# A decoder layer in float32: feed-forward loop with one cyclic order for each engine, scores of two heads as 64-row pairs in two parts, softmax by head, projections up to 1.5 tiles ahead

## Chip, cores and metric

One core of a Trainium2 chip runs the whole program. The metric is the device time of one execution in microseconds (us). Three executions of the kernel before took 1336.63, 1340.5 and 1342.84 us, median 1340.5 us.

## What is computed

Input x has 4 batch rows of 512 positions and 256 features. Three blocks with residuals follow each other: causal self-attention with 16 heads, linear cross-attention with a context, and a feed-forward block of two layers, in which each layer is local attention plus a gated MLP. Only the last block is touched here:

```python
def local_attention(q, k, v):          # windows of 128, each sees itself and the one before
    sim = jnp.einsum('bhwid,bhwjd->bhwij', bq * QK_SCALE, look_around(bk))
    sim = jnp.where(mask, -jnp.finfo(sim.dtype).max, sim)
    return jnp.einsum('bhwij,bhwjd->bhwid', jax.nn.softmax(sim, -1), look_around(bv))

def _layer(x, ...):                    # twice
    q, k, v = split(shift_token(x) @ wqkv)          # 8 heads of 64
    q, k = rotary_xpos(l2norm(q) * qs, l2norm(k) * ksc)
    x = x + local_attention(q, k, v) @ wo
    h = layernorm(shift_token(x)) * lg + lb
    a, g = split(h @ w1 + b1)                       # 2 x 682
    return x + (a * gelu(g)) @ w2 + b2
```

## The kernel before, in words

The program is one list of instructions for each engine, with semaphores between them. The feed-forward block has STEPS = 8 tiles m, one for each layer and batch row (m = 4 layer + batch row), of 512 positions in T = 4 windows t of 128. The work on a tile:

- `hT`: y transposed, split in a rounded part (`hT_hi`) and the rest (`hT_lo`), so that three fp32r matmuls give nearly a float32 product.
- `qkv` (m, t, q or k or v): one window's projection, six matmuls of 512 columns in one PSUM bank (`qkv_tile`, L1461 for all matmuls of the helper `product`). For q and k ACT squares it, DVE multiplies with the rotary tables (L1278, L1284), sums the squares (L1288) and takes a maximum (L1291), POOL adds and computes the inverse norms (L663 to L680). For v ACT copies it.
- `Tqk` (m, t): q and k transposed (L1703). ACT copies q, DVE k (`lkT`).
- `S` (unit u): scores of two heads, u = 4 m + j (`local_scores`, L1721). A head's q stands in `lqz`, [features, pair, window, head, position]: 64 rows hold the head, the other 64 are zeros that POOL sets once, so the matmul contracts over 128 rows of keys of both heads. A head's four windows fill two banks (0 and 1), and `for h`, `for k` asks for 0, 1, 0, 1. DVE adds the mask and takes the maximum (L1324), then the negated maximum (L1331).
- `exp` (u) on ACT (L912, four activations for a head), `soft` (u): DVE's reciprocals (L1337) and POOL's products (L655, L658), both heads in one item.
- `T` (u, h): probabilities transposed (L1736), in banks 3 and 4, copied out by ACT and DVE. `AV` (u): the two heads' outputs go to rows 0 to 63 and 64 to 127 of one bank (L1754), ACT copies it to `loT`.
- MLP of the tile: `wo` (two halves, L1769), `stats`, `sh` (the shifted half of y by two products, L1782, L1784), `norm` (POOL), `apply` (DVE, `hn`, L1374, L1378), `hnT` (transposes, L1793), six hidden tiles `w1` with `hid` and `gl`, and `w2` in two halves.

One table, `SLOTS`, orders all of it. It has four strings, one for each unit j of a tile, and names what comes in that unit; the MLP of tile m - 1 and the projections of tile m + 1 stand between the attention parts of tile m:

```python
SLOTS = ("wo_0 v q soft_now k wo_1 S T0 T1 stats sh norm exp AV Tqk apply bias",
         "v soft_now S hnT q k T0 hid_0 hid_1 T1 hid_2 exp Tqk AV", ...)
```

All engines walk the same list `order` (`cross`, then the slots of m = 1 to 6, then `closing`) and each does its share of an item. PSUM banks are dealt out in that order too: `turn` gives the next of a ring, banks 2, 5, 6, 7 for projections, wo, w1, w2, sh and AV, 3 and 4 for transposes. `wait_free` makes PE wait for the reader of a bank's last contents, `wait_full` a reader for PE. The weights of layer 1 are loaded in one DMA into `wqkv_next`, which shares memory with other buffers, and split on ACT and DVE (`weights`).

Of the kernel before, what the change touches and what calls it, by code (L numbers as in the profile page):

```python
# [14 lines left out]
P = 128  # L15
# [28 lines left out]
GELU_T = 2  # L44

# [35 lines left out]
def build(nc, a, out, x2_dram):  # L81

    with ExitStack() as ctx:
# [99 lines left out]
        shift = sbt(ctx, "shift", [P, 2, P])  # L183
        hn = sbt(ctx, "hn", [P, T, D])
        hnT_hi = sbt(ctx, "hnT_hi", [P, E2, S], F32R)
# [5 lines left out]
        raw = ExitStack()  # L191
        wqkv_next = sbt(raw, "wqkv_next", [P, E2, 3 * INNER])
        raw.close()
# [24 lines left out]
        lqz = sbt(ctx, "lqz", [P, FPAIRS, T, 2, P])  # L218
# [79 lines left out]
        def take(key, bank):  # L298
# [6 lines left out]
        SET1 = 3  # L305
# [4 lines left out]
        WO_PART = ("wo_0", "wo_1", "stats")  # L310
        SLOTS = ("wo_0 v q soft_now k wo_1 S T0 T1 stats sh norm exp AV Tqk apply bias",
# [3 lines left out]

        def slot(m, j):

            u = m * FPAIRS + j
            names = SLOTS[j].split()
            if m == B - 1 and j == 0:  # L320
                names = ["weights", *WO_PART] + [n for n in names if n not in WO_PART]
            if j == 0 and m % B == 1 and m > B:
                names = ["w1_parts"] + names
            items = []
            for name in names:
                if name in ("v", "q", "k"):
                    items.append(("qkv", m + 1, j, name))
                if name in ("Tqk", "Tqk_before"):
                    items.append(("Tqk", m + 1, j - (name == "Tqk_before")))
                if name == "hT" and m + 2 < STEPS:  # L330
                    items.append(("hT", m + 2))
                if name in ("S", "exp", "soft"):
                    items.append((name, u + 1))
                if name == "soft_now":
                    items.append(("soft", u))
                if name in ("T0", "T1"):
                    items.append(("T", u, int(name[1])))
                if name == "AV":
                    items.append(("AV", u))
# [5 lines left out]
                if name == "weights":  # L345
                    items.append((name, 1))
# [1562 lines left out]
```

## Time and profile before

| | |
|---|---|
| median of three executions | 1340.5 us |
| profiled execution: time | 1342.08 us |
| profiled execution: span of the instructions | 1340.3 us |
| PE, weight loads, DVE, ACT, POOL: busy share | 92%, 70%, 65%, 53%, 44% |
| mean granted clock of TensorE | 0.981 of full speed |

The span is cut up by an engine's records; a record's start and length are measured, matmuls are pipelined and overlap their neighbours, so the distance from start to start is what a matmul costs in a row of them. A float32 matmul has two records, an fp32r matmul one. "Idle before" is time in which an engine had nothing running, put down to the one that released it.

### The profile page before, as it was taken

To read this page: it belongs to the slowest core of one execution; us is meant where nothing else is said; L and a number is where in the kernel's file an instruction comes from. 1 tells how busy PE (TensorE), PEld (TensorE's weight loads), DVE (VectorE), ACT (ScalarE), POOL (GpSimd) and SP (SyncE) were. 2 spreads that over 40 slices of the span, in tenths; PEclk is the share of its full clock that TensorE was granted. 3 is DMA by queue.
4 is the path that set the end of the run, shared out by engine and by line. 5 is a ranking of instruction groups with operands and counts; after the bars stand their busy time and mean duration, and the time that the engine had idled before them with its cause. 6 is when DMAs were issued, how large, how long until landed. Compare 5 with 4: busy or idle time off the path is not lost.

```text
span 1340.3 us, 20468 instructions
## 1 busy us (share of the span) xinstructions
PE 1230.4 (92%) x6672; PEld 943.7 (70%) x6672; DVE 875.3 (65%) x2443; ACT 710.9 (53%) x1728; POOL 593.3 (44%) x649
## 2 busy tenths in 40 slices
PE   5899999999998999877799999899999899998978
PEld 4777777777776667565577867777777677776666
DVE  7677777787773656867675585665665955755341
ACT  3677667666662342535456456374465563653531
POOL 1444445444442111466655365355463653652320
PEclk9999999999999999889899999999999999999999
DMA  6222122211223100230000000100001000001010
GB/s 212 48 49 67 37 47 71 48 41 38 48 63 127 32 1 4 68 103 1 1 1 1 0 1 0 48 1 1 17 6 62 1 1 0 2 23 40 1 48 16
DMA packets 31083, 46.09 MB, mean 34 GB/s; under 512 B 4540, under 2 KB 19600, under 8 KB 30992
## 3 DMA queue, kind: packets, MB, share of 16 engines
q1 hardware_dynamic: 30992, 44.98, 11.7%
q8 instruction: 44, 0.72, 0.2%
q14 instruction: 47, 0.39, 0.1%
HBM read 24.00 MB, written 4.19 MB: 21 GB/s over the span
## 4 chain that ended last, share of the span: by engine, by line
PE 32%; issue 21%; DVE 18%; POOL 14%; ACT 13%; DMA 0%; DVEq 0%; POOLq 0%; ACTq 0%
PE psum L1461 19%; POOL probs L621 12%; ACT lp L912 7%; PE psum L1721 4%; PE psum L1754 3%; DVE ra L1278 2%; DVE lp L1324 2%; DVE rb L1284 2%; DVE ss L1288 2%; PE psum L1736 2%; PE psum L1769 1%; DVE lpT L1342 1%; PE psum L1703 1%; ACT sq L897 1%; DVE ss L1291 1%
## 5 line engine op out<-in xcount | busy, mean ns | idle before, releaser
L621 POOL TENSOR_TENSOR probs<-probs,rden 128x128 f32<-128x128 f32 (+3 forms) x256 | 177.4, 729 | 211.7 <-DVE rden L1056 211.7
L912 ACT ACTIVATE lp<-lp,lneg,rn 128x256 f32<-128x256 f32 (+1 forms) x256 | 143.3, 562 | 36.3 <-DVE lneg L1331 36.2
L778 ACT ACTIVATE probs<-probs,negmax 128x128 f32<-128x128 f32 (+3 forms) x256 | 140.6, 554 | 22.6 <-DVE negmax L1051 22.6
L1721 PE MATMUL psum<-lkT,lqz 128*128 128x256 f32 (+1 forms) x512 | 119.4, 375 | 19.9 <-DVE lmax L1324 17.6
L1721 PEld LDWEIGHTS psum<-lkT,lqz 128*128 128x128 f32 x512 | 83.0, 195 | 49.5 <-DVE lmax L1324 38.4
L663 POOL TENSOR_TENSOR ra<-ra,rb 128x512 f32<-128x512 f32 x32 | 42.5, 1327 | 156.6 <-DVE rb L1284 156.6
L1324 DVE CUSTOM_DVE_ANT_0 lp<-psum,local 128x256 f32<-128x256 f32 (+1 forms) x256 | 87.1, 385 | 37.4 <-PE psum L1721 36.3
L1044 DVE CUSTOM_DVE_ANT_0 probs<-psum,causal 128x512 f32<-128x512 f32 (+3 forms) x256 | 110.0, 486 | 2.2 <-issue 1.1
L667 POOL TENSOR_TENSOR rn<-ss,neg_half 128x8 f32<-128x8 f32 x64 | 105.4, 1647 | 5.5
L658 POOL TENSOR_TENSOR lp<-lp,lrden 128x768 f32<-128x768 f32 x64 | 97.6, 1524 | 0.0
L743 ACT ACTIVATE lpT<-psum 128x512 f32<-128x512 f32 x64 | 38.4, 600 | 105.6 <-PE psum L1736 105.6
L1461 PE MATMUL psum<-q,k_rest 128*128 128x256 f32 (+2 forms) x256 | 88.4, 357 | 4.6 <-DVE rowmax L1044 3.0
L1527 PE MATMUL psum<-ident,probs 128*128 128x128 f32 x640 | 90.7, 273 | 1.7 <-POOL probs L621 1.6
L1736 PE MATMUL psum<-ident,lp 128*128 128x128 f32 x448 | 68.3, 287 | 22.1 <-DVE lpT L1342 9.9
L1461 PE MATMUL psum<-hnT_lo,w_hi 128*114 128x512 f32 (+1 forms) x192 | 80.2, 418 | 7.6 <-DVE hnT_lo L1310 7.1
L1461 PE MATMUL psum<-w,hid 114*128 114x256 f32 (+1 forms) x384 | 85.4, 379 | 1.1 <-DVE hid L1388 1.1
L655 POOL TENSOR_TENSOR lp<-lp,lrden 128x128 f32<-128x128 f32 x64 | 25.6, 400 | 137.0 <-DVE lrden L1337 137.0
L1461 PE MATMUL psum<-wqkv_hi,hT_lo 128*128 128x512 f32 x192 | 82.3, 429 | 0.7 <-ACT oxT L743 0.7
L1736 PEld LDWEIGHTS psum<-ident,lp 128*128 128x128 f32 x448 | 53.7, 146 | 39.4 <-DVE lpT L1342 14.5
L1461 PEld LDWEIGHTS psum<-w,hid 114*128 114x128 f32 (+1 forms) x384 | 71.8, 190 | 11.2 <-DVE hid L1388 1.5
L1527 PEld LDWEIGHTS psum<-ident,probs 128*128 128x128 f32 x640 | 74.1, 141 | 6.8 <-POOL probs L621 2.1
L1461 PE MATMUL psum<-q,k 128*128 128x256 f32 (+2 forms) x256 | 78.6, 324 | 0.0
(165 smaller groups left out, 3128.1 us busy)
## 6 DMA issues: line engine op xcount, KB each, us to landing
k<-k_round SPq DMA_DIRECT2D x128, 128.0 KB, 2.4
x<-in_x SPq DMA_DIRECT2D x8, 512.0 KB, 6.1
aw<-in_w_quads SPq DMA_DIRECT2D x4, 768.0 KB, 5.0
w_raw<-in_w SPq DMA_DIRECT2D x2, 1364.0 KB, 6.5
ctxT<-in_ctxT SPq DMA_DIRECT2D x4, 512.0 KB, 3.6
x_scratch<-x SPq DMA_DIRECT2D x4, 512.0 KB, 3.7
x<-x_scratch SPq DMA_DIRECT2D x4, 512.0 KB, 5.6
wqkv_raw<-in_wqkv SPq DMA_DIRECT2D x1, 1536.0 KB, 10.1
```

The lines of the kernel that those rows point to most:

```text
L621: ins = pool.tensor_tensor(pr, pr, rden[:, j % 2, h, i:i + 1].broadcast_to([P, TRI[i]]), ALU.mult)
L658: pool.tensor_tensor(pr, pr, r, ALU.mult).then_inc(l_prob, 1)
L663: pool.tensor_tensor(q3, q3, rb[:, 0, :], ALU.add).then_inc(l_q, 1)
L667: pool.tensor_tensor(rn[:, m % 2, t, i, :], ss[:, i, :], neg_half[:, 0:FH], ALU.pow).then_inc(l_rn, 1)
L778: ins = act.activation(pr, pr, ACT.Exp, bias=negmax[:, j % 2, h, i:i + 1], scale=ADH ** -0.5, accum_out=den[:, j % 2, h, i:i + 1])
L912: ins = act.activation(pr, pr, ACT.Exp, bias=lneg[:, u % 2, h, w:w + 1], scale=rn[:, m % 2, w, 0, 2 * j + h:2 * j + h + 1], accum_out=lden ...
L1044: ins = dve.tensor_tensor_reduce(probs[:, j % 2, h, TRI_AT[i]:TRI_AT[i + 1]], bank[:, at:at + TRI[i]], causal[:, S - TRI[i]:S], 1.0, -3e38 ...
L1324: ins = dve.tensor_tensor_reduce(lp[:, u % 2, h, lo:hi], bank[:, at:at + hi - lo], local[:, LOC - (hi - lo):LOC], 1.0, -3e38, ALU.add, ALU ...
L1461: ins = mm(dst, lhsT, rhs, start=i == 0, stop=i == len(pairs) - 1, **kw)
L1527: ins = pe.transpose(bank[:, at:at + P], probs[:, j % 2, h, lo:lo + P], ident[:, :])
L1721: ins = mm(bank[:, at:at + n].rearrange("p (w k) -> p w k", k=P), lqz[:, c, d, h, :], keys, start=True, stop=True)
L1736: ins = pe.transpose(bank[:, at:at + P], lp[:, u % 2, h, lo:lo + P], ident[:, :])
```

## The change

Five things are changed in the feed-forward loop.

1. **Orders.** `SLOTS` goes. Each engine gets its own string for one step, which is repeated for every tile; `@1` means tile m + 1, `@-1` the tile before. PE's order alone deals out the PSUM banks.
2. **Scores.** `lqz` becomes `lqT`, with the two heads of a pair in rows 0 to 63 and 64 to 127 and no zeros. The matmuls of the two heads alternate, each on its 64 rows, into bank 0 (first head) and 1 (second). A unit has two parts: `Sa` (windows 0 and 1) and `Sb` (2 and 3), which stand apart in the order.
3. **Softmax by head.** `exp` and `soft` are items of one head (`ea`, `eb`, `fa`, `fb`).
4. **Lead.** In a step of tile m, PE also does q, k of windows 0 and 1 of tile m + 2, v of its windows 0 and 1, and the first scores of tile m + 1. Within a window q comes first, then k and v.
5. **Small ones.** One copy of a query tile where there were two; L1291's maximum as a `scalar_tensor_tensor`; layer 1's projection weights in three loads, two to their own memory, v's to that of `hn`.

```diff
-        SLOTS = ("wo_0 v q soft_now k wo_1 S T0 T1 stats sh norm exp AV Tqk apply bias",
...
+        STEP_PE = ("v2@1 hnT@-1 q2@1 Ta1 k2@1 Tb1 Sa3 hid0@-1 Tqk1@1 hid1@-1 Sb3 hid2@-1 hid3@-1 q3@1 "
...
+        def order_of(cycle):
+            middle = [item for m in range(-2, STEPS + 2) for item in step_items(cycle, m) if item not in placed]
+            return cross + middle + closing
+        pe_order, dve_order, act_order, pool_order = (
+            order_of(cycle) for cycle in (STEP_PE, STEP_DVE, STEP_ACT, STEP_POOL))
...
-            if what == "S":
-                for h in range(2):
-                    take(("S", at[0], h, 0), 0)
-                    take(("S", at[0], h, 1), 1)
+            if what in ("Sa", "Sb"):
+                take(("S", at[0], 0, what), 0)
+                take(("S", at[0], 1, what), 1)
...
-                dst = lqz[:, t] if m % 2 else lqz[:, :, t]
-                copy(dst[0:FDH, :, 0, :], src[0:FDH])
-                copy(dst[FDH:P, :, 1, :], src[FDH:P]).then_inc(read[use[0]], 1)
+                dst = lqT[:, t] if m % 2 else lqT[:, :, t]
+                copy(dst, src).then_inc(read[use[0]], 1)
...
-                dve.tensor_scalar(ss[:, i, :], ss[:, i, :], NORM_EPS ** 2, None, ALU.max).then_inc(l_ssm, 1)
+                dve.scalar_tensor_tensor(ss[:, i, :], ss[:, i, :], NORM_EPS ** 2, ss[:, i, :], ALU.max, ALU.max)\
+                    .then_inc(l_ssm, 1)
...
-                for h in range(2):
-                    for k in range(2):
-                        use = plan["S", u, h, k]
-                        bank = wait_free(pe, use)
-                        at = 0
-                        for w in (2 * k, 2 * k + 1):
...
-                            ins = mm(bank[:, at:at + n].rearrange("p (w k) -> p w k", k=P), lqz[:, c, d, h, :], keys,
-                                     start=True, stop=True)
+                pair = [wait_free(pe, plan["S", u, h, part]) for h in range(2)]
+                at = 0
+                for w in WINDOWS[part]:
...
+                    for h in range(2):
+                        rows = slice(h * FDH, (h + 1) * FDH)
+                        ins = mm(pair[h][:, at:at + n].rearrange("p (w k) -> p w k", k=P), lqT[rows, c, d, :],
+                                 keys[rows], start=True, stop=True)
```

PE's instructions around a unit's scores in a step of layer 0 (`waits read0` is the wait for the reader of bank 0, `l_prob` that for POOL's probabilities). Before, behind the second half of wo:

```order
L1769 MATMUL psum<-wo,loT 128x256 x7
L1721 MATMUL psum<-lkT,lqz 128x128 [waits read0]
L1721 MATMUL psum<-lkT,lqz 128x256
L1721 MATMUL psum<-lkT,lqz 128x256 [waits read1]
L1721 MATMUL psum<-lkT,lqz 128x256
L1721 MATMUL psum<-lkT,lqz 128x128 [waits read0]
L1721 MATMUL psum<-lkT,lqz 128x256
L1721 MATMUL psum<-lkT,lqz 128x256 [waits read1]
L1721 MATMUL psum<-lkT,lqz 128x256
L1736 MATMUL psum<-ident,lp 128x128 [waits read3,l_prob]
L1736 MATMUL psum<-ident,lp 128x128 x3
```

After the change, at another unit of the same tile; L1755 and L1737 are the AV and the transposes of before, L1721 is again the scores:

```order
L1461 MATMUL psum<-wqkv_hi,hT_hi 128x512
L1721 MATMUL psum<-lkT,lqT 128x128 [waits read1,read0]
L1721 MATMUL psum<-lkT,lqT 128x128
L1721 MATMUL psum<-lkT,lqT 128x256 x2
L1755 MATMUL psum<-lpT,lv 64x256 [waits read2,read4,read3]
L1755 MATMUL psum<-lpT,lv 64x256 x5
L1755 MATMUL psum<-lpT,lv 64x128 x2
L1721 MATMUL psum<-lkT,lqT 128x256 [waits read1,read0]
L1721 MATMUL psum<-lkT,lqT 128x256 x3
L1737 MATMUL psum<-ident,lp 128x128 [waits read3,l_prob]
L1737 MATMUL psum<-ident,lp 128x128 x3
```

A unit's four fills in a row, with a wait for a bank before each, have become two groups with AV between them, each waiting for both banks.

DVE between the second addition of a tile's wo (L1348) and its normalized rows (L1374, L1378), before; left out are the repeated reads of the same unit's other windows and head:

```order
L1348 TENSOR_TENSOR y<-psum,y 128x512 [waits full5]
L1324 ISA lp,lmax<-psum,local 128x128 [waits full0]
L1324 ISA lp,lmax<-psum,local 128x256
L1331 SCALAR_TENSOR_TENSOR lneg<-lmax,rn 128x4 [waits read1,read0]
L1342 COPY lpT<-psum 128x384 [waits full4] x2
L1356 BN_STATS stats<-y 128x6 [waits read5]
L1362 BN_STATS stats<-psum 128x6 [waits full6]
L1297 COPY lkT<-psum 128x512 [waits full4]
L1374 TENSOR_SCALAR hn<-psum,mv,rstd 128x128 [waits f_rstd,f_mv]
L1378 TENSOR_SCALAR hn<-y,mv,rstd 128x128 x4
L1337 RECIPROCAL lrden<-lden 128x4 [waits l_exp] x2
```

And after, where L1320 is the read of the scores and L1296 the copy of transposed keys:

```order
L1348 TENSOR_TENSOR y<-psum,y 128x512 [waits full5]
L1342 COPY lpT<-psum 128x384 [waits full4]
L1356 BN_STATS stats<-y 128x6 [waits read5,read2]
L1362 BN_STATS stats<-psum 128x6 [waits full7]
L1342 COPY lpT<-psum 128x384 [waits full4]
L1337 RECIPROCAL lrden<-lden 128x4 [waits l_exp]
L1320 ISA lp,lmax<-psum,local 128x128 [waits full0]
L1374 TENSOR_SCALAR hn<-psum,mv,rstd 128x128 [waits f_rstd,f_mv]
L1378 TENSOR_SCALAR hn<-y,mv,rstd 128x128 x4
L1296 COPY lkT<-psum 128x4x128 [waits full4]
L1337 RECIPROCAL lrden<-lden 128x4 [waits l_exp]
```

The two units' scores between have become one part of a unit, and a reciprocal stands ahead of it and of the next.

## Rows read from the trace of the kernel before

**Rows 1.** The page, part 1: busy time (share of the span) and instructions.

```profile
PE 1230.4 (92%) x6672; PEld 943.7 (70%) x6672; DVE 875.3 (65%) x2443; ACT 710.9 (53%) x1728; POOL 593.3 (44%) x649
```

**Rows 2.** Windows: start:end, length, busy us (instructions) by engine, clock, DMA, GB/s.

```profile
589.60:669.25 79.65, 62.08 (x328) 47.30 (x327) 52.21 (x150) 42.73 (x108) 47.23 (x38) 0.91 0.00 1
669.25:759.60 90.35, 86.33 (x462) 67.15 (x461) 57.66 (x158) 49.13 (x113) 46.37 (x42) 1.00 0.00 1
849.83:943.59 93.76, 87.58 (x462) 68.37 (x460) 60.94 (x161) 51.95 (x116) 46.38 (x42) 0.98 0.00 1
1214.81:1283.87 69.06, 59.68 (x294) 44.32 (x292) 30.78 (x105) 35.62 (x87) 25.56 (x25) 0.93 0.00 1
```

**Rows 3.** Groups in 669.25 to 1214.81: busy us, mean ns | idle before, releaser.

```profile
L912 ACT ACTIVATE lp<-lp,lneg,rn 128x256 f32<-128x256 f32 x193 | 108.1, 562 | 18.6 <-DVE lneg L1331 18.5
L1721 PE MATMUL psum<-lkT,lqz 128*128 128x256 f32 (+1 forms) x385 | 87.6, 368 | 10.8 <-DVE lmax L1324 10.3
...
L1736 PE MATMUL psum<-ident,lp 128*128 128x128 f32 x336 | 50.1, 282 | 10.8 <-DVE lpT L1342 8.4 <-ACT lpT L743 2.3
...
L1291 DVE TENSOR_SCALAR ss<-ss 128x8 f32<-128x8 f32 x48 | 38.1, 794 | 1.6
```

**Rows 4.** Timeline of PE, one step: start us, us, what [idle before].

```profile
770.63 1.68 PE L1721 MATMUL psum<-lkT,lqz 128*128 128x128 f32 x8
...
786.87 1.04 PE L1793 MATMUL psum<-ident,hn 128*128 128x128 f32 x8
...
820.73 3.79 PE L1721 MATMUL psum<-lkT,lqz 128*128 128x128 f32 x16
824.36 1.04 PE L1703 MATMUL psum<-ident,ra 128*128 128x128 f32 x8
```

**Rows 5.** Timeline of PE, the same step.

```profile
777.09 1.02 PE L1782 MATMUL psum<-y,shift 128*128 128x512 f32 x2
...
778.69 1.73 PE L1754 MATMUL psum<-lpT,lv 128*64 128x256 f32 x16
...
801.20 1.03 PE L1703 MATMUL psum<-ident,ra 128*128 128x128 f32 x8
802.17 1.73 PE L1754 MATMUL psum<-lpT,lv 128*64 128x256 f32 x16
803.83 0.50 PE L1461 MATMUL psum<-wqkv_hi,hT_lo 128*128 128x512 f32 x1
...
809.83 0.39 PE L1461 MATMUL psum<-wqkv_hi,hT_lo 128*128 128x512 f32 x1
...
811.22 0.93 PE L1736 MATMUL psum<-ident,lp 128*128 128x128 f32 x7
...
830.25 5.35 PE L1461 MATMUL psum<-w,hid 114*128 114x256 f32 x24
```

**Rows 6.** Instructions of L1754 (AV): what its engine's idle time waited for, us, times.

```profile
  issue: 14.3, 32
```

**Rows 7.** Timeline of DVE, the same step.

```profile
771.39 0.68 DVE L1348 TENSOR_TENSOR y<-psum,y 128x512 f32<-128x512 f32 x1
771.99 0.27 DVE L1324 CUSTOM_DVE_ANT_0 lp<-psum,local 128x128 f32<-128x128 f32 x1
...
772.54 0.08 DVE L1324 DVE_READ_ACCUMULATOR2_ANT lmax<- 128x1 f32 x1
...
782.09 1.36 DVE L1374 TENSOR_SCALAR hn<-psum,mv,rstd 128x128 f32<-128x128 f32 x4
783.36 1.11 DVE L1378 TENSOR_SCALAR hn<-y,mv,rstd 128x128 f32<-128x128 f32 x4
```

**Rows 8.** Timeline of the tail, after the last AV.

```profile
1288.32 0.69 DVE L1348 TENSOR_TENSOR y<-psum,y 128x512 f32<-128x512 f32 x1 [0.17 <-PE psum L1769]
...
1292.64 1.04 POOL L687 TENSOR_TENSOR rstd<-rstd,neg_half 128x4 f32<-128x4 f32 x1
```

**Rows 9.** Waits of DVE in 669.25 to 1214.81: us in total, times, longest.

```profile
DVE lrden L1337 <- ACT lp L912: 32.6, 18, 2.1
```

More of the change, by code:

```diff
@@ L304, in build @@
         STEPS = DEPTH * B
[L305 removed]
+        SET1 = 2
         UNITS = STEPS * FPAIRS
[L310 to L311 removed]
[3 rows of a table removed]
[L316 to L323, printed above, removed]
[L324 to L348 removed]
@@ new lines, in build, with step_items @@
+        STEP_POOL = ("bias k3@2 fb2@1 fa3@1 fb3@1 q0@3 k0@3 fa0@2 q1@3 fb0@2 k1@3 norm@1 fa1@2 fb1@2 q2@3 "
+                     "k2@3 fa2@2 q3@3")
+        MLP = ("stats", "sh", "norm", "apply", "hnT", "hT", "bias")
+        def step_items(cycle, m):
+            items = []
+            for token in cycle.split():
+                name, _, lead = token.partition("@")
+                n = m + int(lead or 0)
+                what = name[:2] if name[:2] == "w2" else name.rstrip("012345")
+                i = int(name[len(what):] or 0)
+                u = n * FPAIRS + i
+                if not 0 <= n < STEPS:
+                    continue
+                if what in ("q", "k", "v"):
+                    items.append(("qkv", n, i, what))
+                if what in ("Sa", "Sb", "AV"):
+                    items.append((what, u))
+                if what in ("ea", "eb", "fa", "fb", "Ta", "Tb"):
+                    items.append(({"e": "exp", "f": "soft", "T": "T"}[what[0]], u, "ab".index(what[1])))
+                if what in ("Tqk", "wo", "hid", "w2"):
+                    items.append(({"hid": "w1"}.get(what, what), n, i))
+                if what in MLP:
+                    items.append((what, n))
+                if what == "weights" and n == B:
+                    items.append((what, 1))
+                if what == "tab" and n == B:
+                    items.append((what, 1))
+                if what == "wparts" and n % B == 0:
+                    items.append(("w1_parts", n // B))
@@ L396, in turn @@
             turns[which] += 1
-        for what, *at in order:
+        for what, *at in pe_order:
             if what == "awo":
@@ L713, in final_sum @@
                 pool.tensor_tensor(y[:, b, :, :], y[:, b, :, :], x2[:, b, :, :], ALU.add).then_inc(fin_done, 1)
-            for what, *at in order:
+            for what, *at in pool_order:
                 if what == "norm2":
@@ L952, in gates @@
                                bias=b1[0:rows, m // B, 1, f:f + 1]).then_inc(read[use[0]], 1)
-            for what, *at in order:
+            for what, *at in act_order:
                 if what == "x1T":
@@ L1389, in hidden @@
                                          gl[0:rows, f % GELU_T, :], ALU.add, ALU.mult).then_inc(read[use[0]], 1)
-            for what, *at in order:
+            for what, *at in dve_order:
                 if what == "awo":
@@ L1683, in qkv_tile @@
                 if t == 0:
-                    if what == "v":
+                    if what == "q":
                         for e in range(E2):
@@ L1820, in second_part @@
                 ins.then_inc(full[use[0]], 1)
-            for what, *at in order:
+            for what, *at in pe_order:
                 if what == "awo":
```

204 lines of the change are left out of this document (102 added, 102 removed), and 29 rows, old and new, of tables (SLOTS, STEP_DVE, closing, cross).

## Prediction

> **What bounds the kernel now.** I read the totals first. TensorE (PE) is busy for 1230.4 us, 92% of the span, the next engine, VectorE (DVE), for 875.3 us [rows 1]. That is an average over two stages, so I cut the feed-forward loop into its steps by the first output projection of each. A step takes 90.35 us, of which PE is busy for 86.33 and DVE for 57.66, ScalarE (ACT) for 49.13, POOL for 46.37 [rows 2]. In six such steps, 545.6 us from 669.25 to 1214.81, PE is the bound and nothing else is within 30 us a step of it. The ramp ahead of them (79.65 us, PE busy 62.08) and the part from 1214.81 to the last AV (69.06 us, PE busy 59.68) are different: there PE waits for chains through the other engines.
>
> Then, what PE does in the six steps [rows 3]. The local scores (L1721) have 385 matmul records, 87.6 us busy, and 10.8 us of idle time just ahead of them, nearly all until DVE has freed a score bank. They are 24 units (a unit is one pair of heads of one batch row), so a unit costs 98.4 / 24 = 4.1 us. The transposes of the probabilities (L1736) show 50.1 us busy and another 10.8 us idle, until DVE or ACT has copied the previous transposes out. All else together waits for some 6 us. So a step has about 4.5 us of PE idle, and its other 86 us go only if PE gets less work.
>
> **The paired scores.** Now a head's queries stand in 64 of 128 rows with zeros in the others, and each matmul takes the whole array. A unit that meets no wait takes 824.36 - 820.73 = 3.63 us for 16 records [rows 4]. After the change the two heads sit in rows 0 to 63 and 64 to 127, in alternate matmuls and in different banks; the number and width of the matmuls stay. What a pair on row halves costs, the trace does not show. Its nearest relative is AV (L1754), whose two heads use two halves of the array's columns, with the same 16 records of the same widths: 803.83 - 802.17 = 1.66 us [rows 5]. Had they gone one after the other, at the pace of w2's 256-wide records (5.35 us for 24, 0.22 each [rows 5], half for the 128-wide), they would take 12 x 0.22 + 4 x 0.11 = 3.08 us. So pairs do overlap, and 1.66 us is 0.12 above the ideal half, 1.54; I read this as going in and out of the divided array, and count 0.15. The scores differ from AV in one respect: each load is 128 columns wide, not 64. Eight transposes, each with a 128-wide load and a 128-wide matmul, take 802.17 - 801.20 = 0.97 us, 0.121 each [rows 5]. If loads of two row halves don't overlap, 16 of them are 1.94 us. With 0.15 for each of the two parts a unit comes to 2.24 us. The bounds are 1.66 (like AV) and 3.63 (no overlap). I take **2.24**, because the load is the part of which there is a row: a gain of 1.39 us a unit. For the 24 units of the six steps that is **33.3 us**, for the eight units outside them **11.1 us**. At 1.66 the gain would be 18.6 us more, at 3.63 all 44.4 are gone.
>
> The trace shows 14.3 us of idle, 32 times, charged to "issue" ahead of AV's loads and matmuls, 0.45 us a unit [rows 6], though only about 0.15 us of it reaches the pace. The Trainium skill, "TensorEngine Tiling (Array Packing)", section Tiling Modes, speaks against the change here: changing the tiling mode drains TensorE, and the change adds four such switches a unit. What a full drain would do is the second rival.
>
> **The waits on banks.** Before, PE asks for four score fills of two banks in a row, so the third waits for DVE. In the new order two parts of a unit have at least one AV or one hidden tile between them, and both transposes of a unit are set apart too. DVE needs 0.55 to 0.7 us for a bank (771.99 to 772.54 for the narrower [rows 7]), and AV alone gives 1.66. So in the six steps I let 9 of the 10.8 us ahead of the scores go, and 7 of the 10.8 ahead of the transposes; what stays is late probabilities. **16 us.** Zero is the lower end, 21.6 the upper.
>
> **The other edits.** ACT copies a query tile once and not twice, DVE's 8-column maximum in another form (L1291, 38.1 us for 48 in the six steps, 0.79 each [rows 3]): both engines are 30 us a step below PE, so nothing, save in the ramp. The clearing of the zero-padded queries on POOL goes; it lies beside PE's work in the cross-attention, nothing. The split of layer 1's projection weights costs PE 93.76 - 90.35 = 3.4 us now, in its one step [rows 2]. In the change PE has hT, half of w2 (24 records at 0.22, 5.2 us [rows 5]) and Tqk between the split and the first tile that needs it. Covered, 3.4 us are won; if ACT's copies stay ahead of everything, none: I take the middle, **1.7 us**. No queue is put behind a longer wait on SP: the loads stand there in the order in which their memory comes free.
>
> **The lead and the private orders.** In the ramp PE is idle for 79.65 - 62.08 = 17.6 us. Four more projection tiles (six records each, 811.22 - 809.83 = 1.39 us [rows 5]) and one more score unit are done there, beside waits for softmax; that is work off PE's later path: **4 us** (bounds 0 and 8). In return the last tile has no projections left to fill its waits. PE's work from the last output projection of tile 6 to the last AV is then mostly chains; PE is idle there for 9.4 us now, and I add **3 us** (0 to 8). In the steady steps the private order must not bring new stalls. The tightest place is between the second output projection of a tile (wo) and the transposes of its normalized rows (hnT). PE's work between them falls from 16.2 us (770.63 to 786.87, two score units with their waits in it [rows 4]) to v 1.39, shift 1.6, T 0.85 (7 x 0.121), v 1.39, two score parts 2.24, AV 1.66, Tqk 0.97, v 1.39 = 11.5 us [rows 5]. The chain itself: in the tail, where DVE has nothing else of weight, 1288.32 to 1293.68 from the addition to POOL's power [rows 8], and the application 782.09 to 784.47 [rows 7], together 7.7 us; DVE has one copy, a reciprocal and one score part (1.5 us) between, so 9.5 to 10. It fits, by a microsecond or two. So nothing, but see the third rival.
>
> **Sum.** 33.3 + 11.1 + 16 + 1.7 + 4 - 3 = 63 us off the profiled execution of 1342.1 us: 1279. Its time is 1.6 us above the median of the runs (1340.5), which is within what they scatter; I leave the forecast at **1279 us**. A step would take about 82.7 us, against PE's work of 86.4 - 5.6 = 80.8.
>
> **The rivals.** First, the **pairs overlap like AV and the ramp fills well**: 18.6 + 4 us more, 1256. For it: all 16 loads of an AV fit into its 1.66 us. It lies in the forecast's own range. The Trainium skill, "TensorE: Matmul & The Clock Gate", Part 3, has it so: matmuls on distinct row groups run concurrently, and a load overlaps a running matmul only where the row groups differ; no trace here shows it for rows. Second, the **pairs win nothing**. If each of the four switches a unit costs the whole 0.45 us of rows 6, a unit is 1.94 + 1.8 = 3.74 us, as before. The 44.4 us are gone, 1323 remains. Against it: after AV the next projection starts 1.66 us later, so the idle time before the loads was mostly hidden. It is also the case in which the change doesn't do what it says. Third, **the chain to hnT is late**. It took 771.39 to 784.47 us, 13.1, in the step shown [rows 7], because DVE had a whole unit's scores inside it. If it takes as long with 11.5 us of cover, PE stalls 2 to 4 us in each of eight tiles: 1279 + 24 = 1303. Against it: the new order of DVE has less in between. Fourth, **slower**: DVE becomes the bound through its own waits. Its order now has eight single reciprocals a step (soft, by head), each waiting for ACT's exponentials of a head, which take four activations of 0.56 us, 2.2 us [rows 3], and which in turn wait for DVE. DVE's work is 57.7 us a step, so this decides from 90.9 - 57.7 = 33 us of waits that hide nothing. At 42 us a step is 99.7 us, six steps are 53 us longer, and the outside gains of 12 us are kept: 1342 + 53 - 12 = 1383. At 36, 1347. For it: even now DVE waits for 32.6 us in six steps for these sums [rows 9], but that is 5.4 a step; 36 is far off.
>
> **How the numbers follow.** The forecast, 1255 to 1296 with the unit at 1.66 to 2.7 us, gets 0.66. Late hnT, 1296 to 1310: 0.13. Pairs that win little or nothing, 1310 to 1330: 0.13. No change, when both the second rival and the waits come back: 0.03. Slower: 0.05. A measurement of this kernel tells 0.5% from no change, 6.7 us. So faster 0.92, same 0.03, slower 0.05. The range must leave out 2 in 10: it starts at 1252, a little under the first rival (which takes in the upper ends of waits and ramp), and ends at 1316, into the second.
>
> **What would show it.** In the new profile: L1721 at some 72 us busy (32 x 2.24) and not 119.4, steps of 81 to 84 us, PE idle ahead of scores and transposes under 10 us in the six steps. A unit of two parts at 3 us or more, or part to part with loads idle between, speaks for the second rival; idle time of PE ahead of hnT or the first hidden tile for the third; DVE idle until ACT's accumulations in sum above 30 us a step for the fourth. I am wrong if steps are above 87 us or below 78.

## Result, and the profile after

| | before | after |
|---|---|---|
| executions, us | 1335.9 to 1342.8 (4) | 1258.2 to 1260.5 (4) |
| median, us | 1338.6 | **1258.9** |
| ratio, 95% interval | 1 | 0.940 (0.938 to 0.942) |
| profiled execution: time, span, us | 1342.1, 1340.3 | 1258.9, 1257.1 |
| mean granted clock | 0.981 | 0.986 |

The change takes 80 us off; 63 were forecast. Busy time by engine, of the kernel after:

```profile
PE 1168.3 (93%) x6672; PEld 893.2 (71%) x6672; DVE 840.2 (67%) x2443; ACT 686.9 (55%) x1696; POOL 587.9 (47%) x648
```

PE lost 62.1 us of work [rows 1] and 21.1 us of idle time; together these are the 83.2 us of the span. The same stages as in rows 2, cut at the first output projection (wo) of a tile. The kernel after, windows (start:end, length, busy us by engine, clock, DMA, GB/s): the ramp, an ordinary step, the step with the weights, and the part from the last step to the last AV.

```profile
590.13:672.06 81.93, 61.11 (x377) 44.44 (x375) 60.14 (x179) 43.08 (x113) 55.67 (x48) 0.92 0.05 16
751.81:833.30 81.49, 79.48 (x462) 61.50 (x461) 57.67 (x161) 48.93 (x112) 47.74 (x42) 1.00 0.02 8
833.30:913.04 79.74, 79.12 (x462) 61.61 (x461) 52.32 (x158) 46.10 (x109) 45.78 (x42) 1.00 0.00 1
1146.41:1198.70 52.29, 45.18 (x259) 33.16 (x257) 24.93 (x91) 33.61 (x81) 23.84 (x23) 1.00 0.03 11
```

Against [rows 2]: the ramp is 2.3 us longer, an ordinary step 10.6 us shorter (79.74 for 90.35), with 0.62 us of PE idle left in it where there were 4.0; the last part is 16.8 us shorter. Some of this is work that now stands behind it: from 1146.41 to the end the kernel after takes 110.7 us, the kernel before, from 1214.81, 125.5, so 14.8 us less. The six steps (672.06 to 1146.41) take 474.35 us for 545.56, 71.2 less. In these, the groups of PE that changed (busy us, mean ns, idle before them and its releaser):

```profile
L1721 PE MATMUL psum<-lkT,lqT 64*128 64x256 f32 (+1 forms) x384 | 49.5, 376 | 0.0
L1737 PE MATMUL psum<-ident,lp 128*128 128x128 f32 x338 | 47.1, 276 | 4.0 <-ACT hnT_hi L941 3.7 <-ACT lqT L745 0.3
L1461 PE MATMUL psum<-wqkv_hi,hT_lo 128*128 128x512 f32 x136 | 58.2, 428 | 0.0
```

The scores have 38.1 us less work than in [rows 3] and none of their 10.8 us of waiting. The transposes wait 4.0 us, for 10.8. The third row is one of the three kinds of projection matmul; it has 136 records where the kernel before has 144 in its six steps: the lead has moved four projection tiles, 24 records, into the ramp. PE's whole idle time in the six steps is 5.4 us, for 27.5.

A piece of the ordinary step on PE's timeline (start, us, what, idle before in brackets), to be held against rows 4 and 5:

```profile
833.30 7.07 PE L1770 MATMUL psum<-wo,loT 128*128 128x256 f32 x32
...
845.34 0.93 PE L1721 MATMUL psum<-lkT,lqT 64*128 64x128 f32 x8
846.20 1.74 PE L1755 MATMUL psum<-lpT,lv 128*64 128x256 f32 x16
847.86 1.13 PE L1721 MATMUL psum<-lkT,lqT 64*128 64x256 f32 x8
848.93 1.09 PE L1703 MATMUL psum<-ident,ra 128*128 128x128 f32 x8
...
851.25 1.04 PE L1794 MATMUL psum<-ident,hn 128*128 128x128 f32 x8
...
854.78 0.55 PE L1737 MATMUL psum<-ident,lp 128*128 128x128 f32 x3 [0.62 <-ACT hnT_hi L941]
```

The reader should take the distance from start to start. The first part of a unit is 846.20 - 845.34 = 0.86 us, the second 848.93 - 847.86 = 1.07: a unit costs **1.93 us**, AV between them still 1.66. The transposes of the normalized rows (L1794) start without a wait. The 0.62 us at 854.78 is the only idle stretch of the step.

### The profile page after: what moved, and what is told of

Read it like the earlier page. It is cut to its first block, busy times and chain, and to the rows that moved or that the text cites. A ratio compares the mean times of both kernels' runs of the same rounds, so it can differ in the third digit from the quotient of the medians.

```text
span 1257.1 us, 20486 instructions
## 1 busy us (share of the span) xinstructions
PE 1168.3 (93%) x6672; PEld 893.2 (71%) x6672; DVE 840.2 (67%) x2443; ACT 686.9 (55%) x1696; POOL 587.9 (47%) x648
## 4 chain that ended last, share of the span: by engine, by line
PE 53%; issue 20%; POOL 15%; DVE 7%; ACT 4%; DMA 0%; POOLq 0%; DVEq 0%; ACTq 0%
PE psum L1461 33%; POOL probs L625 13%; PE psum L1721 5%; PE psum L1770 4%; PE psum L1755 4%; PE psum L1737 4%; PE psum L1703 2%; ACT hnT_hi L941 1%; DVE stats L994 1%; ACT hnT L941 1%; POOL rn L669 1%; DVE ra L1276 1%; PE psum L1783 1%; DVE rb L1282 1%; DVE xn L1003 1%
## 5 line engine op out<-in xcount | busy, mean ns | idle before, releaser
L911 ACT ACTIVATE lp<-lp,lneg,rn 128x256 f32<-128x256 f32 (+1 forms) x256 | 143.8, 571 | 17.6 <-DVE lneg L1332 17.4
L1320 DVE CUSTOM_DVE_ANT_0 lp<-psum,local 128x256 f32<-128x256 f32 (+1 forms) x256 | 84.0, 383 | 22.8 <-PE psum L1721 22.8
L660 POOL TENSOR_TENSOR lp<-lp,lrden 128x768 f32<-128x768 f32 x64 | 95.0, 1484 | 0.0
L665 POOL TENSOR_TENSOR ra<-ra,rb 128x512 f32<-128x512 f32 x32 | 41.0, 1280 | 93.0 <-DVE rb L1282 93.0
L898 ACT ACTIVATE sq<-psum 128x512 f32<-128x512 f32 x64 | 38.1, 598 | 80.0 <-PE psum L1461 73.4
L1388 DVE SCALAR_TENSOR_TENSOR hid<-psum,b,gl 114x512 f32<-114x512 f32 (+1 forms) x48 | 36.0, 750 | 67.3 <-PE psum L1461 53.9
L745 ACT ACTIVATE pT<-psum 128x512 f32<-128x512 f32 (+1 forms) x96 | 49.3, 515 | 57.2 <-PE psum L1527 57.2
L1721 PE MATMUL psum<-lkT,lqT 64*128 64x256 f32 (+1 forms) x512 | 67.8, 384 | 12.5 <-DVE lmax L1320 9.3
L1543 PE MATMUL psum<-pT,v 128*64 128x256 f32 (+3 forms) x512 | 76.0, 439 | 2.3 <-ACT pT L745 1.7
```

The costliest lines, as they stand in the source:

```text
L660: pool.tensor_tensor(pr, pr, r, ALU.mult).then_inc(l_prob, 1)
L911: ins = act.activation(pr, pr, ACT.Exp, bias=lneg[:, u % 2, h, w:w + 1], scale=rn[:, m % 2, w, 0, 2 * j + h:2 * j + h + 1], accum_out=lden ...
L1320: ins = dve.tensor_tensor_reduce(lp[:, u % 2, h, lo:hi], bank[:, at:at + hi - lo], local[:, LOC - (hi - lo):LOC], 1.0, -3e38, ALU.add, ALU ...
L1543: ins = mm(bank[rows, c * P:S], v[:, b % 2, c, cols], pT[:, h, KEYB_AT[c]:KEYB_AT[c] + KEYB[c]], start=c == 0, stop=c == T - 1)
L1721: ins = mm(pair[h][:, at:at + n].rearrange("p (w k) -> p w k", k=P), lqT[rows, c, d, :], keys[rows], start=True, stop=True)
```

## The experiments

All runs are of the whole program, at least four executions each; medians and ratios against the kernel before, timed beside them.

| run | edit | us | ratio (95%) |
|---|---|---|---|
| after | | 1258.9 | 0.940 (0.938, 0.942) |
| e7_full_rows | scores on all 128 rows | 1289.8 | 0.962 (0.958, 0.966) |
| e8_same_rows | both heads on rows 0 to 63 | 1308.7 | 0.974 (0.971, 0.978) |
| e1_heads_in_turn | heads not alternating | 1262.0 | 0.942 (0.938, 0.946) |
| e2_before_paired | kernel before, pairs alone | 1367.5 | 1.021 (1.016, 1.026) |
| e3_parts_adjacent | Sb right behind Sa | 1297.3 | 0.971 (0.965, 0.977) |
| e4_one_order | one order for all engines | 1319.1 | 0.984 (0.981, 0.987) |
| e11_act_follows | ACT on the common order | 1274.0 | 0.950 (0.948, 0.952) |
| e12_act_pool_follow | ACT, POOL on it | 1275.8 | 0.952 (0.950, 0.954) |
| e10_dve_act_follow | DVE, ACT on it | 1313.3 | 0.979 (0.977, 0.982) |
| e6_old_max | L1289 as before | 1258.9 | 0.939 (0.936, 0.942) |
| e5_ramp | DVE's order in the ramp | 1254.8 | 0.937 (0.933, 0.940) |
| e9_ramp_act | and ACT's | 1255.2 | 0.937 (0.935, 0.939) |

### What the pairs are worth: e7_full_rows

```diff
-                        rows = slice(h * FDH, (h + 1) * FDH)
-                        ins = mm(pair[h][...], lqT[rows, c, d, :], keys[rows], start=True, stop=True)
+                        ins = mm(pair[h][...], lqT[:, c, d, :], keys, start=True, stop=True)
```

> The changed kernel, whose score matmuls take all 128 rows again (queries and keys of both heads, so the scores come out as the sum over both heads, which is left so; number, width, banks and order of the instructions are those of the change). Theory (the pairs carry most of the gain, and PE is the bound): a unit costs 3.62 us again in place of 0.86 + 1.06 = 1.92, 1.7 us for each of the 24 units of the six steps and most of the other eight, 41 to 54 us: 1300 to 1313 us, a step 79.7 + 6.8 = 86.5 us. Rival (the orders and parts carry it): under 1280 us.

It took 31 us more than the kernel after, less than the forecast allowed. On its timeline of PE, the two parts of a unit:

```profile
841.47 1.47 PE L1720 MATMUL psum<-lkT,lqT 128*128 128x128 f32 x8
842.87 1.74 PE L1754 MATMUL psum<-lpT,lv 128*64 128x256 f32 x16
844.53 1.99 PE L1720 MATMUL psum<-lkT,lqT 128*128 128x256 f32 x8
846.36 0.93 PE L1736 MATMUL psum<-ident,lp 128*128 128x128 f32 x7
```

Here a unit is 1.40 + 1.83 = 3.23 us. One unit in four has a hidden tile behind each part, and there it is 1.12 + 1.54 = 2.66, but this is mostly a shift: the first fp32r record starts 0.03 us behind the last score record, where a transpose starts 0.22 behind it, and the next fp32r record is 0.19 us late in return. With this it is 3.04. Over six steps (677.45 to 1177.09, 499.64 us, 25.3 more than after) the pairs are worth 1.05 us a unit, so a unit on the whole array, with free banks, counts for some 3.0 us.

The 3.63 us of [rows 4] must be held against 3.14: the 3.23 has the same neighbours (AV ahead, transposes behind), but also AV between its parts, which starts 0.09 us later than a transpose would. So 0.5 us of that stretch was waiting. The timeline of PE's matmuls has no bracket there, and I had read this as the absence of a wait. The timeline of its weight loads (PEld) does have two, in the same unit of the kernel before:

```profile
822.39 0.52 PEld L1721 LDWEIGHTS psum<-lkT,lqz 128*128 128x128 f32 x4 [0.27 <-DVE lmax L1324]
823.39 0.73 PEld L1721 LDWEIGHTS psum<-lkT,lqz 128*128 128x128 f32 x4 [0.48 <-DVE lmax L1324]
```

In its six steps the loads of the scores wait 26.2 us for DVE, in 48 places; the matmuls show 10.3 us in 12.

### Why they are faster: e8_same_rows, e1_heads_in_turn

```diff
-                        rows = slice(h * FDH, (h + 1) * FDH)
+                        rows = slice(0, FDH)
```

> The changed kernel, in which both heads' score matmuls take rows 0 to 63 (so the second head's scores are those of the first, which is left so). Theory (two heads on different halves run at the same time): on one half nothing can overlap, a part costs at least what the 128-row matmuls cost in the run with full rows (1.4 and 1.83 us in place of 0.86 and 1.06), 1285 to 1300 us. Rival (a float32 matmul on 64 rows is faster by itself, which would also be why heads one after the other cost only 3 us): 1259 to 1262 us, parts of 0.86 and 1.06 us.

50 us slower, 9 us above the range of the theory. The parts, on its timeline of PE:

```profile
849.78 1.57 PE L1721 MATMUL psum<-lkT,lqT 64*128 64x128 f32 x8
851.28 1.73 PE L1755 MATMUL psum<-lpT,lv 128*64 128x256 f32 x16
852.95 1.99 PE L1721 MATMUL psum<-lkT,lqT 64*128 64x256 f32 x8
854.87 0.98 PE L1737 MATMUL psum<-ident,lp 128*128 128x128 f32 x7
```

1.50 + 1.92 = 3.42 us a unit, 1.49 more than after; 32 units make 48 of the 50 us. The whole gain of the pairs is that the heads sit on different halves; short contraction alone gives nothing.

It is even slower than all rows, and the comparison with e7_full_rows shows the price of dividing the array. Within a part the records of both runs follow each other at the same pace (0.216 us for a 256-wide one). The difference lies where scores on 64 rows meet work on the whole array. From the start of one record to the starts of the next two it is, in us:

| from, to | 64 rows | all rows |
|---|---|---|
| last score record, two transposes | 0.31 + 0.16 | 0.22 + 0.11 |
| a transpose, two score records | 0.20 + 0.21 | 0.11 + 0.11 |
| last score record, two fp32r records | 0.31 + 0.33 | 0.03 + 0.42 |

So such a change costs 0.15 to 0.20 us. A step has ten of them more than in e7_full_rows (in front of each first part, between scores and transposes three times, and three around the hidden tiles), and the six steps are 510.39 - 499.64 = 10.75 us longer, at the same idle time (5.5 and 5.4 us): 0.18 us for each change, 0.45 us a unit. The pairs pay this too; they win 1.49 us by the overlap and keep 1.05.

The Trainium skill, "TensorE: Matmul & The Clock Gate", Part 3, has the overlap (matmuls on distinct row groups run concurrently), and the trace agrees: 0.86 and 1.07 us against 1.50 and 1.92 for the same records on one half.

```diff
-                for w in WINDOWS[part]:
-                    for h in range(2):
+                for h in range(2):
+                    for w in WINDOWS[part]:
```

> The changed kernel, in which a part's two matmuls of head 0 come first and then those of head 1, still on 64 rows each. Theory (records on the same rows follow each other, only alternating ones overlap): within a part two of the four matmuls overlap at most at the seam, so a unit costs 2.8 to 3.4 us, 0.9 to 1.5 us more than 1.92: 1280 to 1300 us. Rival (64 rows are faster by themselves, or a loaded half need not alternate): no change, 1259 us.

The theory failed: 3 us slower, and its parts are 0.86 and 1.07 us as well. Its six steps take 474.67 us, for 474.35. The 3 us of the profiled execution lie in one place, from the last but one wo (1146.33) to the last, where the granted clock is 0.94 and the stretch takes 52.79 us; in the kernel after it takes 49.61 at 1.00. e9_ramp_act below has the same.

With the four matmuls of a part listed head by head they overlap as much. The first part of a unit lists the first head's 128-wide matmul (two records), then its 256-wide one, then the second head's two. What starts on PE between 845.04 and 845.30 is four 128-wide records, so both heads:

```profile
L1721 PE MATMUL psum<-lkT,lqT x4: 272/322/373, 845.0 to 845.3; 64*128 64x128 f32 x4
```

The second head's records start 13 ns behind the first head's (7 ns in the kernel after), though they are listed behind a 256-wide matmul. What puts them side by side the trace does not show.

### Pairs without the new order: e2_before_paired

The kernel before, with `lqT` and the two heads side by side. DVE's reads of the banks follow PE's new order, and both heads' negated maxima now come behind the last read, where the first head's stood behind its own two; nothing else is changed:

```diff
-                    for k in range(2):
-                        bank = wait_free(pe, plan["S", u, h, k])
+                for k in range(2):
+                    pair = [wait_free(pe, plan["S", u, h, k]) for h in range(2)]
```

> The kernel before with its one order, and only the pairs: queries without zeros, heads alternating on 64 rows each, head 0 in bank 0 and head 1 in bank 1, both parts of a unit one behind the other. Theory (a unit's matmuls shrink to 1.92 us, but the second part now waits until DVE has read both banks, 1.4 us): a unit costs 3.3 us beside 4.1 before, 0.8 us less for 24 units and as much for some of the others: 1312 to 1322 us, and PE idle ahead of L1721 rises from 10.8 to 30 us or more in the six steps. Rival (pairs alone give their 1.7 us a unit): 1285 us.

It is 2% **slower** than the kernel before: both numbers were missed, by 45 us and more. The waits of PE between 670 and 1230 us in that run (us in total, times, longest):

```profile
PE psum L1720 <- DVE lmax L1322: 43.3, 24, 4.8
```

and one unit of it on PE's timeline:

```profile
870.74 0.93 PE L1720 MATMUL psum<-lkT,lqT 64*128 64x128 f32 x8
876.52 2.08 PE L1720 MATMUL psum<-lkT,lqT 64*128 64x256 f32 x8 [4.85 <-DVE lmax L1322]
878.53 1.75 PE L1736 MATMUL psum<-ident,lp 128*128 128x128 f32 x7
```

There the cheaper scores show (0.93 us for eight records), and at once PE waits 4.85 us until DVE has read both banks. Before, PE filled bank 1 while DVE read bank 0; now both banks come full together and are wanted free together, and DVE, whose list still has two projection tiles ahead of this unit (870.51 to 875.19 on its timeline), comes late to the first. The last two rows show a second price: behind the wait the second part takes 2.08 us and the transposes 1.75, where without one they take 1.13 and 0.93. The window from 876.52 to 878.50 has a granted clock of 0.50. The six steps are 17.1 us longer than before, the rest of the 28 us lies in the ramp and the tail. A step is 92.4 us long, 2 longer than before:

```profile
680.47:772.88 92.41, 83.21 (x462) 64.29 (x461) 55.70 (x159) 46.33 (x108) 45.94 (x42) 0.96 0.00 1
```

PE is busy for 83.21 us, 3.1 less than before, idle for 9.2, 5.2 more, and the granted clock is 0.96 instead of 1.00. The pairs moved PE's work into waits, and behind waits the clock was lower. How much of the 28 us is the later maximum of the first head, which the exponentials wait for, no run tells.

### The parts apart: e3_parts_adjacent

```diff
-... Sa3 hid0@-1 Tqk1@1 hid1@-1 Sb3 ...  Sa0@1 AV2 Sb0@1 ... Sa1@1 AV3 Sb1@1 ... Sa2@1 AV0@1 Sb2@1 ...
+... Sa3 Sb3 hid0@-1 Tqk1@1 hid1@-1 ...  Sa0@1 Sb0@1 AV2 ... Sa1@1 Sb1@1 AV3 ... Sa2@1 Sb2@1 AV0@1 ...
```

> The changed kernel, with Sb right behind Sa in PE's order; all other orders stay. Theory (the parts stand apart so that DVE's two reads of 0.7 us, and its start behind other work, are covered): PE waits 1.2 to 2 us in each of 32 units, 38 to 60 us: 1295 to 1315 us, with the idle time ahead of L1721 at 30 us or more. Rival (it was worth what the waits ahead of the scores cost before, 0.45 us a unit): 1270 to 1275 us.

38 us slower, as the theory had it. Its waits of PE in the six steps, and a unit on PE's timeline:

```profile
PE psum L1721 <- DVE lmax L1320: 33.6, 24, 1.5
```

```profile
841.24 0.93 PE L1721 MATMUL psum<-lkT,lqT 64*128 64x128 f32 x8
843.55 1.14 PE L1721 MATMUL psum<-lkT,lqT 64*128 64x256 f32 x8 [1.38 <-DVE lmax L1320]
844.61 1.74 PE L1755 MATMUL psum<-lpT,lv 128*64 128x256 f32 x16
```

Each of the 24 units waits for DVE once, 1.4 us: the 1.66 us of AV, or a hidden tile, between the parts is what hides DVE's read. Without the distance between the parts, more than the 31 us of the pairs is gone.

### Own orders: e4_one_order, e11, e12 and e10

PE's order, pairs, parts and lead stay; the other engines get PE's order with their own items put in where PE makes their input.

```diff
+        STEP = ("v2@1 hnT@-1 q2@1 Ta1 ea2 k2@1 Tb1 eb2 fa2 Sa3 hid0@-1 fb2 Tqk1@1 hid1@-1 Sb3 ... "
...
-            order_of(cycle) for cycle in (STEP_PE, STEP_DVE, STEP_ACT, STEP_POOL))
+            order_of(cycle) for cycle in (STEP, STEP, STEP, STEP))
```

> The changed kernel with one cyclic order for all engines: PE's, with softmax by head, statistics, normalization and bias put in where their inputs are there. Pairs, parts and lead stay. Theory (the gain is in PE's order and the parts; the other engines have 25 us of slack a step): 1262 to 1280 us. Rival (an order of one's own is what keeps DVE and ACT from waiting for each other): 1290 us and more, with PE idle ahead of scores and transposes.

60 us slower, and the rival holds: against this common order, three quarters of the whole gain hangs on the orders of the other engines, which I had costed at nothing. (The prices of the runs overlap and don't add up to the 80 us; another common order might cost less, and none was tried.) The three runs that divide it (the same edit, with STEP for the engines named):

> The kernel after with ACT alone on the common order. In the common order ACT copies the output of AV and v at once where PE makes them, and starts a unit's exponentials later against the projections' squares. Theory: ACT's place of the exponentials is half of the 60 us, because DVE's maxima, ACT's exponentials and PE's transposes are one chain: 1280 to 1300 us. Rival: ACT has 45 percent of idle time in a step and shifts cost nothing: 1257 to 1265 us.

> The kernel after with ACT and POOL on the common order, DVE keeps its own. Against the run with ACT alone the difference is POOL's, against the run with all on one order (1319 us) it is DVE's. Theory: DVE's own order is worth 20 us or more, since DVE holds the reads that free PE's banks: 1280 to 1299 us. Rival: DVE's order counts little, 1305 to 1320 us.

> The kernel after, with DVE and ACT on the common order of the earlier run with one order for all engines, which took 1319 us; PE's is the same in both, POOL keeps its own. The 60 us between that run and the kernel after are to be divided. Theory: they are DVE's and ACT's, since POOL only has the rotary sums, norms and products, in whatever order these arrive: 1305 to 1319 us. Rival: POOL's own order, which takes the products of the probabilities ahead of the sums of the projections, is what counts: below 1290 us.

ACT's own order is worth 15 us, POOL's 2 and 6 (with ACT, where the 2 lie within the scatter, and with ACT and DVE on the common one), DVE's 39 (1313.3 against 1274.0) or 43 (1319.1 against 1275.8). e11 and e12 came out below their theories (1280 to 1300, 1280 to 1299), so ACT's part is a quarter and not half; e10 lies in its theory's range, and DVE's share is above the 20 us expected. PE's waits in the six steps of e10 (684.74 to 1203.08):

```profile
PE psum L1759 <- issue: 10.9, 5, 2.3
PE psum L1741 <- DVE lpT L1346: 8.4, 6, 1.4
PE psum L1725 <- DVE lmax L1324: 7.8, 5, 1.6
PE psum L1798 <- DVE lkT L1300: 5.8, 6, 1.0
PE psum L1741 <- ACT lqT L749: 5.0, 7, 0.8
```

And one of the second kind, on the timeline of all its engines; the other engines' rows are left out:

```profile
884.84 0.60 PE L1741 MATMUL psum<-ident,lp 128*128 128x128 f32 x4
884.86 0.68 DVE L1290 TENSOR_REDUCE ss<-sq 128x8 f32<-128x512 f32 x1
...
885.57 0.75 DVE L1293 SCALAR_TENSOR_TENSOR ss<-ss 128x8 f32<-128x8 f32 x1
...
886.24 0.55 DVE L1346 COPY lpT<-psum 128x384 f32<-128x384 f32 x1
...
886.84 0.55 PE L1741 MATMUL psum<-ident,lp 128*128 128x128 f32 x3 [1.40 <-DVE lpT L1346]
```

The copy that frees the transposes' bank takes 0.55 us, but stands behind the squares' sum and maximum of a projection tile, which PE is not waiting for. DVE is hardly busier in that step than in the kernel after (53.8 us of 88.2, for 52.3 of 79.7); it does the right work in the wrong order. What ended the waits ahead of AV that the profile calls "issue" was not found out.

### The maximum: e6_old_max

```diff
-                dve.scalar_tensor_tensor(ss[:, i, :], ss[:, i, :], NORM_EPS ** 2, ss[:, i, :], ALU.max, ALU.max)\
+                dve.tensor_scalar(ss[:, i, :], ss[:, i, :], NORM_EPS ** 2, None, ALU.max).then_inc(l_ssm, 1)
```

> The changed kernel with the old form of the 8-column maximum (a tensor_scalar of one input). Theory (DVE is off the path in the steps): within 0.3%, 1257 to 1263 us. Rival (it holds DVE or POOL in the ramp, where DVE is the bound): 1264 us and more.

No difference, as the forecast had it.

### The ramp: e5_ramp and e9_ramp_act

The longest wait of PE after the hT of tile 1 is in the ramp of the kernel after:

```profile
618.28 2.08 PE L1721 MATMUL psum<-lkT,lqT 64*128 64x256 f32 x8 [9.33 <-DVE lmax L1320]
```

DVE owes that read, but stands at the reciprocals of unit 0 waiting for ACT, and then computes tables and treats a query tile first.

```diff
-... k3@1 tab@5 fa3 ...
+... k3@1 tab@3 fa3 ...
...
+        dve_order[i:i + 1] = [("Sa", 1), ("soft", 0, 0)]
...
+        dve_order[i:i] = [("soft", 0, 1)]
```

> The changed kernel; on DVE alone the rotary tables of layer 1 are made in tile 1 and not in the ramp, and the two reciprocals of unit 0 come behind the reads of unit 1's first part, not ahead of tile (1, 1) of q. Theory (PE's longest wait, 9.3 us at the second part of unit 1, is for DVE, which waits 4.3 us for ACT's exponentials and spends 3.0 us on the tables): 5 to 8 us less, 1251 to 1254 us. Rival (DVE is full in the ramp, 60.1 of 82 us, so the work comes back behind): 1257 to 1259 us.

4 us faster than after, between theory and rival. The ramp is 78.7 us and the wait 7.11. What is left of it is ACT: the squares of the next tiles stand behind eight exponentials.

```diff
+        early = [("qkv", 1, 1, "q"), ("qkv", 1, 1, "k")]
+        act_order = [item for item in act_order if item not in early]
+        i = act_order.index(("exp", 0, 0))
+        act_order[i:i] = early
```

> The kernel after with two changes of order in the ramp: DVE's as in the run before it (tables of the rotary products loaded earlier in its order, the first reciprocals later), and ACT squares the q and k tile of window 1 of tile 1 ahead of the first exponentials instead of behind them. In the run with DVE's change alone, PE waits 7.11 us at 614.00 for the second scores of unit 1, and DVE 4.99 us for ACT's squares, which stand behind eight exponentials (605.51 to 609.98) though ACT had nothing to do for 1.62 us ahead of these. Theory: the squares fill that gap, DVE's tile comes 5 us earlier, and the wait of 7.1 us shrinks to under 3: 1249 to 1251 us. Rival: the probabilities of unit 0 then set the time of PE's first transposes, which don't move: the ramp stays as long as in the run with DVE's change alone, 1254 to 1256 us.

The wait became what the theory said:

```profile
609.28 1.13 PE L1731 MATMUL psum<-lkT,lqT 64*128 64x256 f32 x8 [1.83 <-DVE lmax L1330]
```

The ramp is 74.7 us, 7.2 shorter than after, and the six steps are as long as before that (474.56 us). Yet the time is that of e5_ramp: the rival's number, but not for its reason, since the ramp did become shorter. In the profiled execution most of the 4 us was given back later, at the last tile. Windows from the seventh tile's wo to the last one's; the kernel after:

```profile
1146.41:1196.02 49.61, 42.50 (x248) 31.07 (x246) 24.38 (x90) 33.15 (x81) 21.52 (x23) 1.00 0.00 1
```

and e9_ramp_act:

```profile
1138.84:1191.38 52.54, 45.50 (x247) 32.62 (x246) 23.89 (x90) 33.25 (x81) 23.04 (x23) 0.94 0.02 5
```

PE's waits there are the same in both, 7.1 us; its work takes 3.0 us longer, at a granted clock of 0.94 for 1.00. The last but one AV shows it, in the kernel after:

```profile
1192.13 1.73 PE L1755 MATMUL psum<-lpT,lv 128*64 128x256 f32 x16 [2.75 <-ACT lpT L745]
```

and in e9_ramp_act:

```profile
1185.93 3.25 PE L1765 MATMUL psum<-lpT,lv 128*64 128x256 f32 x16 [2.75 <-ACT lpT L755]
```

The same wait of 2.75 us, the same 16 records, once at a granted clock of 1.00 and once at 0.50 (2.4 and 1.2 GHz). Why the clock held in one and not in the other the runs don't tell. The two ramp versions are each some 4 us faster than the kernel after, and not to be told from each other; one of e5_ramp's four executions took 1259.4 us.

No run takes out the softmax by head, the lead or the three loads of the weights alone.

## Why the prediction was right, and where its steps were off

**Sign and mechanism: right.** PE was the bound, the gain came as less PE work and as fewer waits ahead of scores and transposes, and no rival that ends above the forecast came true. That the sum comes within 20 us is partly luck: the pairs were put some 13 us too high, and the waits and the tail together by more than that too low. The time, 1258.9, lies in the range and in the forecast's own range, 20 us below the number, next to the first rival (1256), which had "pairs overlap like AV and the ramp fills well". Its first half came nearly true, its second did not.

**The paired unit: mis-sized twice.** I took 2.24 us, on the thought that 16 loads at the pace of 0.121 each would bound it. It measured 1.93, and the eight loads of a part fit into 0.86 us, less than 8 x 0.121: loads of different row halves do overlap. Part of the distance to AV's 1.66 are the switches, for which I had 0.15 us for each of the two parts; e8 against e7 has 0.45 a unit. But the base, 3.63, was too high as well: with free banks a unit on the whole array counts for some 3.0 us (e7). So the pairs alone are worth 31 us, not 44.4. What I booked there beyond that was mostly hidden waiting for banks (0.5 us in the unit that I had read), which the parts apart removed.

**The waits: too small for the steps.** I let 16 us go, 9 of them ahead of the scores. Of the 27.5 us of PE idle in the six steps 22.1 went: all 10.8 ahead of the scores, 6.8 ahead of the transposes (7 forecast), and 3.7 ahead of the hidden tiles, which I had not counted. The 24 units of before take 94.0 us from their first records to what follows, waits in them included, those of e7 74.2: so the score banks were worth some 20 us, for my 9, and half of it had no bracket.

**The private orders: "nothing" was wrong as a price, right as a forecast.** I asked only whether the new orders bring stalls, and they bring none: the chain from wo (its last record is issued just ahead of 840.0) to the transposes of the normalized rows has 851.25 - 840.0 = 11.2 us of cover, against my 11.5, and fits (rival three is false). But what they are worth is 60 us against one common order. The version with everything else of the change came out at 1319 us, near the number of the second rival (1323), for another reason. My sum had the gain of that part without naming it: "two parts of a unit have an AV between them" holds only if DVE reads a part within AV's time, and that is its order's doing.

**The lead: right in size, booked in the wrong place.** The ramp did not become shorter by 4 us but longer by 2.3, because its new score unit meets the 9.33 us wait; PE is idle there for 20.8 us, for 17.6 before. The four projection tiles that it took from the steps save 7.9 us of records there, 5.6 at their pace of 1.39. Net some 3 us, without the score unit that it took off the tail.

**The tail: wrong sign.** I added 3 us; the part up to the last AV is 16.8 us shorter, and the program from the same point to its end 14.8. 8.0 us are the scores (32 records for 49, each cheaper), 2.9 are wo records that now stand behind the last AV, 2.3 idle; the remaining 3.6 are the same matmuls at a granted clock of 1.00 where the window of before has 0.93 [rows 2]. The last I had not counted at all, and e1 and e9 show that it can as well go the other way.

**The weights: right.** That step costs 81.49 - 79.74 = 1.75 us more than an ordinary one, for 3.4: 1.7 won, as booked.

**The four rivals.** Pairs that win nothing: false, a unit is 1.93 us. The switches have a price, but a smaller one: 0.45 us for all that the change adds to a unit (e8 against e7), where that rival had 0.45 for each of four. It adds two and a half a unit on average and not four, since where AV stands between the parts its own two were there before. The Trainium skill, "TensorEngine Tiling (Array Packing)", Tiling Modes, says that changing the mode drains TensorE; the trace agrees that a change costs something, 0.15 to 0.20 us. Late hnT: false. DVE bound by its own waits: false; DVE's waits for the exponentials' sums fell from 32.6 us [rows 9] to 11.9 in the six steps, softmax by head and all:

```profile
DVE lrden L1337 <- ACT lp L911: 11.9, 4, 3.0
```

**The signs that I named.** The scores are 67.8 us busy in all, for "some 72"; steps are 79.7 us, for 81 to 84; PE idle ahead of scores and transposes 4.0 us, for "under 10".

## What to carry to other kernels

Making the bounding engine's work cheaper can be worth nothing until its partners can follow: here the pairs are worth 31 us with the new orders and, in the order of before, cost 28. When a resource changes hands in two steps (fill, read), put other work of the filler between two fills of it, at least as long as the read takes, and order the reader by who waits for it and not by when its input comes. And before a stretch of a timeline is taken as an operation's price, it should be held against the same stretch elsewhere and against the weight loads' own timeline: a wait of a load may have no bracket on the matmuls. The neighbours must be the same too.

## What the runs showed of the hardware that was not expected

- Two float32 score matmuls on different halves of the rows cost what one costs: 1.93 us for 16 records. On the same half 3.42 us, on all rows 2.66 to 3.23. It did not matter whether the heads alternate in the list: e1 lists them one after the other, and their records still start 13 ns apart.
- A matmul on 64 rows is not cheaper than one on 128: 0.216 us for a 256-wide record on either. A part on 64 rows is dearer by its switches: 1.50 and 1.92 us, against 1.12 to 1.40 and 1.54 to 1.83.
- A change between the undivided array and 64-row work costs 0.15 to 0.20 us, seen in the starts of the first two records behind it (e8 against e7).
- An fp32r record starts 0.03 us behind a float32 one on the whole array, and the record behind it is 0.19 us late; at such a seam the distance from start to start alone misleads.
- PE's work behind a wait can take twice its time. After the 9.33 us wait in the ramp the second part took 2.08 us instead of 1.13, at a granted clock of 0.50, after 4.85 us in e2 likewise; after 2.75 us once 3.25 us for 16 records and once 1.73. So a removed wait can be worth more than its length, and a shift by some us can cost what it won.
